# Convolution products added on VectorE before TensorE transposes them; the transposed k in another PSUM bank

## The reference

```python
x = x + tanh(g_xattn) * xattn(ctx, ctx, layernorm(x), ssm_kernel, D)
x = x + tanh(g_ffn) * ffn(layernorm(x), ...)
# xattn, per head h of 8 rows: kv[i,j] = ctx[i] * ctx[j]
#   y[i,j] = causal convolution of kv[i,j] with ssm_kernel[h] (length 512) + D[h] * kv[i,j]
#   out[j] = sum over i of y[i,j] * q[i]
# ffn: y = silu(two-tap convolution); q = silu(y Wq), k = y Wk, v = y Wv, g = y Wg
#   rotary on q and k; a two-way router from v picks the half of q and k that is kept
#   o = (q k^T, masked) v;  out = (silu(g) * normalised o) Wout
```

## Time and profile before

| | |
|---|---|
| median of 3 runs | 1015.58 us (1014.01 to 1015.77) |
| profiled execution, its own time | 1016.0 us |
| its span | 1014.2 us |
| mean granted TensorE clock | 0.981 |
| busy: PE, PEld, DVE, ACT, POOL | 930.4, 790.7, 627.9, 426.9, 672.9 us |

### The profile page before, as it was taken

The page is one execution under the profiler, slowest core; times in us unless marked ns, Lnnn a source line. Parts: engine busy times, 40 slices in busy tenths (PEclk is TensorE's granted clock), DMA queues, the critical chain, the costliest instruction groups (busy, mean ns, idle before and its releaser), DMA issues.

```text
span 1014.2 us, 18862 instructions
## 1 busy us (share of the span) xinstructions
PE 930.4 (92%) x7168; PEld 790.7 (78%) x7168; DVE 627.9 (62%) x1400; ACT 426.9 (42%) x906; POOL 672.9 (66%) x613
## 2 busy tenths in 40 slices
PE   1599999999999999999999999999999999999983
PEld 1488888888888888888888888888888878888862
DVE  4766666657666665666666567666656756656542
ACT  2454444444444444434444443444444444444220
POOL 6677667777666677766667776666777666676321
PEclk9889999999999999999999999999999999999986
DMA  8101222112222210222221022222101222210000
GB/s 275 59 30 44 58 58 58 28 31 58 59 58 58 58 32 28 57 59 58 58 58 32 28 57 59 58 59 58 37 24 56 58 59 58 58 37 9 9 12 21
DMA packets 25992, 52.50 MB, mean 52 GB/s; under 512 B 2544, under 2 KB 3696, under 8 KB 25904
## 3 DMA queue, kind: packets, MB, share of 16 engines
q1 hardware_dynamic: 22304, 46.59, 17.1%
q10 hardware_dynamic: 3600, 4.72, 1.4%
HBM read 42.75 MB, written 8.55 MB: 51 GB/s over the span
## 4 chain that ended last, share of the span: by engine, by line
PE 81%; DMA 5%; issue 4%; POOL 4%; DVE 3%; ACT 2%; SPq 0%; POOLq 0%; ACTq 0%
PE bank L315 34%; PE bank L289 19%; PE bank L276 10%; PE bank L265 8%; DMA x_in<-in_x 4%; PE bank L301 3%; PE bank L347 3%; PE bank L333 3%; ACT gate_sb L583 2%; POOL o_rstd L635 1%; DMA w_all<-in_L_ffn_Wv 1%; POOL rstd L635 1%; POOL rot_b L658 1%; DVE gated L827 0%; POOL kv_low L629 0%
## 5 line engine op out<-in xcount | busy, mean ns | idle before, releaser
L629 POOL TENSOR_TENSOR kv_low<-kv,kv_high 128x576 fp32r<-128x576 f32 x128 | 182.0, 1433 | 162.2 <-ACT kv_high L479 162.2
L289 PE MATMUL bank<-kv_high,toep 128*128 128x512 f32 x640 | 225.2, 409 | 11.0 <-DVE z_terms L732 5.6
L620 POOL TENSOR_TENSOR kv<-kx 128x512 f32<-128x512 f32 x128 | 159.2, 1244 | 6.7 <-DMA const<-shape_consts 6.7
L289 PEld LDWEIGHTS bank<-kv_high,toep 128*128 128x128 f32 x640 | 123.0, 192 | 42.1 <-DVE z_terms L732 12.1
L635 POOL TENSOR_TENSOR o_rstd<-o_ve,minus_half 128x16 f32<-128x16 f32 x32 | 93.1, 2911 | 81.7 <-DVE o_ve L802 81.7
L479 ACT ACTIVATE kv_high<-kv 128x576 fp32r<-128x576 f32 x128 | 87.6, 687 | 101.8 <-POOL kv L623 101.8
L289 PE MATMUL bank<-kv_low,toep 128*128 128x512 f32 x320 | 127.4, 398 | 0.0
L315 PE MATMUL bank<-w_all_high,yT_high 128*128 128x512 f32 (+2 forms) x512 | 120.5, 357 | 1.8 <-DVE gated L827 1.8
L880 DVE TENSOR_TENSOR out_sb<-bank,x 128x512 f32<-128x512 f32 x32 | 22.1, 692 | 159.0 <-PE bank L315 159.0
L276 PEld LDWEIGHTS bank<-const,z_terms 128*128 128x128 f32 x1024 | 113.8, 141 | 5.5 <-ACT qx L468 1.2
L276 PE MATMUL bank<-const,z_terms 128*128 128x128 f32 x1024 | 117.0, 273 | 1.0 <-ACT qx L468 1.0
(11 more groups left out here) (101 smaller groups left out, 1650.5 us busy)
## 6 DMA issues: line engine op xcount, KB each, us to landing
toep<-taps_dram SPq DMA_DIRECT2D x32, 512.0 KB, 7.1
kx<-in_ctx SPq DMA_DIRECT2D x32, 384.0 KB, 7.5
x_in<-in_x SPq DMA_DIRECT2D x32, 256.0 KB
out_x<-out_sb SPq DMA_DIRECT2D x32, 256.0 KB
w_all<-in_L_ffn_Wv ACTq DMA_DIRECT2D x1, 1024.0 KB, 12.6
w_all<-in_L_ffn_Wg ACTq DMA_DIRECT2D x1, 1024.0 KB, 11.3
w_out<-in_L_ffn_Wout ACTq DMA_DIRECT2D x1, 1024.0 KB, 17.1
router<-in_L_ffn_router_w ACTq DMA_DIRECT2D x1, 512.0 KB, 7.3
```

The lines of the kernel that those rows point to most:

```text
L289: ins = nc.tensor.matmul(bank[lc % 2][:, :], toep[:, 1 - p, a, (lc - mc) * P:(lc - mc + 1) * P], kv_p[b][:, 1 - p, mc, 0:FULL], start=(mc ...
L620: eng.tensor_tensor(view(kv[:, c % 2, 0:FULL], [[ROW, NROT], [1, ROW]]), view(kx[:, p, c, 0:ROW], [[0, NROT], [1, ROW]]), view(kx[:, p, c, ...
L629: eng.tensor_tensor(kv_p[1][:, p, c, :], kv[:, c % 2, :], kv_p[0][:, p, c, :].bitcast(F32), ALU.subtract).then_inc(kv_ready[c], 1)
```

## The change

- On DVE, a new function add_halves adds the upper four blocks of z_terms to the lower four, in place: once for chunks 0 and 1 together (right behind u, ahead of line 827), and once each for chunks 2 and 3 (behind multiply of chunk 3, ahead of ratio).
- PE's add_transposed does four transposes a chunk and waits for the sums.
- PE transposes gated ahead of add_transposed, and ACT copies gatedT ahead of the high parts of kv chunks 2 and 3.
- The transposed k goes to bank 7, where gatedT was: PE transposes q first, without waiting for the gate, then waits for gatedT_ready (line 870) and transposes k. The wait for the gate moves to the scores. ACT copies q first, then k. The z transposes wait for the copy of k instead of gatedT_ready.

```diff
@@ tensor: add_transposed
                 for c in range(CH):
-                    if c == 0:
-                        eng.wait_ge(mul_last, h1 + 1)
-                    eng.wait_ge(mul_done[c], h1 + 1)
-                    for i in range(2 * NROT):
+                    eng.wait_ge(sum_done[max(c, 1)], h1 + 1)
+                    for i in range(NROT):
                         ins = nc.tensor.matmul(bank[2][:, c * P:(c + 1) * P], z_terms[:, c, i * ROW:(i + 1) * ROW], ident,
-                                               is_transpose=True, start=(c == 0 and i == 0), stop=(i == 2 * NROT - 1),
+                                               is_transpose=True, start=(c == 0 and i == 0), stop=(i == NROT - 1),
                                                skip_group_check=True)
@@ tensor: scores
+                    eng.wait_ge(qeT_sb, h + 1)
                     eng.wait_ge(keT_sb, h + 1)
-                    eng.wait_ge(qeT_sb, h + 1)
+                    eng.wait_ge(gate_ready, h + 1)
@@ tensor: step
                     eng.wait_ge(z_ready, h + 1)
-                    if can_wait(h - 1):
-                        eng.wait_ge(gatedT_ready, h - 1)
+                    if can_wait(h):
+                        eng.wait_ge(keT_sb, h)
                     transpose4(bank[7], lambda c: z[:, c * P:(c + 1) * P], zT_ps)
...
+                if tail:
+                    eng.wait_ge(gated_ready, h)
+                    if back:
+                        eng.wait_ge(y_conv, h + 1)
+                    else:
+                        eng.wait_ge(keT_sb, h)
+                    transpose4(bank[7], lambda c: gated[:, c * P:(c + 1) * P], gatedT_ps)
                 if front:
                     if pre:
                         eng.wait_ge(qx_ready, h + 3)
                     add_transposed(h + 1)
-                if tail:
-                    eng.wait_ge(gated_ready, h)
-                    if back:
-                        eng.wait_ge(y_conv, h + 1)
-                    transpose4(bank[7], lambda c: gated[:, c * P:(c + 1) * P], gatedT_ps)
...
                     eng.wait_ge(qke_ready, h + 1)
-                    eng.wait_ge(gate_ready, h + 1)
-                    transpose4(bank[5], lambda c: qke[:, RH + 4 * c:RH + 4 * c + 4, :], keT_ps)
                     transpose4(bank[3], lambda c: qke[:, 4 * c:4 * c + 4, :], qeT_ps)
+                    if tail:
+                        eng.wait_ge(gatedT_ready, h)
+                    transpose4(bank[7], lambda c: qke[:, RH + 4 * c:RH + 4 * c + 4, :], keT_ps)
@@ scalar: step (kv_round 2 and 3 now stand behind the copy of gatedT; the copy of qeT ahead of that of keT)
-                if pre:
-                    kv_round(p, 2, h + 2)
-                    kv_round(p, 3, h + 2)
                 if tail:
                     eng.wait_ge(gatedT_ps, h)
...
+                if pre:
+                    kv_round(p, 2, h + 2)
+                    kv_round(p, 3, h + 2)
@@ vector
+            def add_halves(chunks, h1):
+
+                eng.wait_ge(mul_last, h1 + 1)
+                eng.wait_ge(mul_done[chunks.stop - 1], h1 + 1)
+                half = NROT * ROW
+                eng.tensor_tensor(z_terms[:, chunks, 0:half], z_terms[:, chunks, 0:half], z_terms[:, chunks, half:2 * half],
+                                  ALU.add).then_inc(sum_done[chunks.stop - 1], 1)
...
+                if front:
+                    add_halves(slice(0, 2), h + 1)
                 if tail:
                     eng.wait_ge(o_rstd_ready, h)
...
                 if front:
                     multiply(p, 3, h + 1)
+                    add_halves(slice(2, 3), h + 1)
+                    add_halves(slice(3, 4), h + 1)
```

More of the change, by code:

```diff
@@ L194, in flamingo_gated_layer @@
         y_low, gatedT_ready = sem("y_low"), sem("gatedT_ready")
+        sum_done = [sem(f"sum_done{i}") for i in range(CH)]
         (mul_last, y_conv, out_ready, ad_ready, u_ready, th1_ready, rth1_ready, ratio_ready, eps_ready,
@@ L592, in step @@
                 if back:
-                    eng.wait_ge(keT_ps, h + 1)
+                    eng.wait_ge(qeT_ps, h + 1)
                     if can_wait(h):
@@ L596, in step @@
                             eng.wait_ge(attn_ps[r], h)
-                    eng.activation(keT[:, :, :], bank[5][:, :].rearrange("p (c n) -> p c n", c=CH), ACT.Copy
-                                   ).then_inc(keT_sb, 1)
-                    eng.wait_ge(qeT_ps, h + 1)
                     eng.activation(qeT[:, :, :], bank[3][:, :].rearrange("p (c n) -> p c n", c=CH), ACT.Copy
                                    ).then_inc(qeT_sb, 1)
+                    eng.wait_ge(keT_ps, h + 1)
+                    eng.activation(keT[:, :, :], bank[7][:, :].rearrange("p (c n) -> p c n", c=CH), ACT.Copy
+                                   ).then_inc(keT_sb, 1)
             run(eng, step)
```

## The result

The changed kernel takes 1001.27 us (median of 4 runs, 996.31 to 1001.56) against 1015.29 us before: ratio 0.9852, interval [0.9835, 0.9869]. It is 14 us faster, where 27 us slower was forecast.

The account below looks back on a forecast made before the run. PE's program and its waits bound the kernel; after the change POOL's path, 2.2 us longer, decides: 14.33 + 16.1 gives about 30.45 us a step, 0.94 more, +27.3 over 29 steps, -1 at the ends: 1042 us, range 1007 to 1056.

Parts of the forecast that it names:

- the price of the sum of chunks 0 and 1: On DVE behind u: o_rstd on POOL holds the 1024-column sum off until its end, costing 1.1 us a step.
- the forecast step (30.45): One step of the changed kernel: 14.33 us up to T plus 16.1 to the scores, 0.94 over 29.51.
- The small sums: DVE sums of chunks 2 and 3 beside busy POOL: 0.55 us each, 1.1 us on POOL's path, no gain possible.
- part A: Stretch of a step from scores to T (last masks, convolutions, statistics): stays 14.33 us.
- PE alone: PE's own program: 16 fewer transposes save 1.75 us, the dropped gate wait 0.78, together 2.53 us a step.
- v at T + 1.9: PE's start of v, behind the delayed sum and line 827 on DVE: 1.9 us after T instead of 0.78.
- T: The end of POOL's o_rstd, the point where the prediction cuts each step in two.
- the first rival: o_rstd leaves room for the large sum, which costs nothing: step 29.3 us, kernel 1010 us; chance 0.17.
- A wait for line 870: PE, ahead of transposing k, waits 1.55 us for gatedT_ready from DVE, in place of the gate's wait.
- PE waits for the copies ahead of the scores: POOL's rstd ends 2.2 us later, so ACT's copies do too; PE waits 0.9 us a step for them.
- The clock: Rival: PE, idle 3.55 of 30.45 us, loses clock: 1130 us; chance 0.05, shared with another new wait.
- part B: Stretch of a step from T to the scores, 15.10 us before; forecast 16.1, under the first rival 14.95.

Follow-up runs that it names:

- the probe: Changed kernel plus one unused 256-column DVE addition, both inputs in SBUF, asked just after o_rstd starts on POOL: one run, 999.43 us.
- run 6: Changed kernel with the sum of chunks 0 and 1 moved on DVE from behind u to behind the reciprocal, beside POOL's rotation: 1039.17 us, 1.0227 of the kernel before.
- the reordering alone: The change without its sums (32 transposes kept; k in bank 7, new PE and ACT orders): 984.54 us, 0.9702 of the kernel before.
- run 4: Changed kernel with the root of x2 on POOL moved ahead of the low parts of chunks 2 and 3: 962.63 us, 0.9486 of the kernel before.
- Run 7: Kernel of run 4 with the load of x issued ahead of the store of the output: 961.31 us, 0.9466 of the kernel before.

## Why the prediction was wrong

**The step that failed** is the price of the sum of chunks 0 and 1: "I take 1.1 us". It was booked at the upper of its two bounds, 1.1 us; it cost nothing, which was the lower. I chose by the nearest rows, rot_a holding line 832 off to its end and a root waiting for DVE. The second showed that a root that asks while DVE runs waits for it, and I read it the other way round as well, that a running root keeps DVE off. The sum itself denies that, with its 1.21 us inside o_rstd, and so does the probe: 0.17 us into a root, a DVE instruction of two SBUF inputs ran at once.

Of the 1.44 us between the forecast step (30.45) and the measured one (29.01) this is 1.1. The small sums at 0.86 us instead of 1.1 are 0.24, and part A is 0.13 shorter; with roundings that is all of it.

By the Trainium skill (SBUF — State Buffer, "SBUF: two separate sides") the one that starts first has the pair of ports that the two engines share for the whole instruction. Rot_a and the rotation of run 6 agree; the long root does not, with 0.41 us for the probe, and the measurement decides.

**Point by point.**
- PE alone shorter by 2.53 us a step: right. Its busy time fell by 53.4 us, and the reordering alone, for which I had 0.78, made the step 29.51 - 28.52 = 0.99 us shorter.
- v at T + 1.9: wrong, T + 0.86, as the first rival had it.
- The two small sums lengthen POOL's path by 1.1 us, no gain possible: the mechanism right, the size 0.86. The root of x2 ends at 485.21 + 0.54 = 485.75, and T of that step is 502.26 - 28.99 = 473.27: T + 12.48, where before had 518.48 - 506.86 = 11.62.
- A wait for line 870 (now 885) in the gate's place: right, but 0.79 us, not 1.55.
- PE waits for the copies ahead of the scores: right, 1.28 us, forecast 0.9.
- The order on POOL and ACT decides rather than PE's end: right, and proved by run 4.
- The clock did not fall: 0.980 after, 0.981 before, with 2.1 us of PE waiting a step. It did in run 6. The prediction called an idle share of 3.55 in 30.45 us half of 2.96 in 15; it is 0.6 of it.
- The first rival's 29.3 us and 1010 us were 0.3 us a step too long: part B 14.8 us, forecast 14.95, and part A 14.20 for 14.33. Both differences are tenths, and 28 steps of them are 8 us, which carried the result out at the fast end of the range.
- "Part A stays 14.33, as its instructions are the same": wrong by 0.13, most of it the landing of x. In the typical step before, the statistics of x start 500.84 - 500.05 = 0.79 us behind line 780, after the change 496.25 - 495.56 = 0.69 behind line 791, its counterpart. Run 7 against run 4, an edit of the x load alone, takes the same tenth off (median 0.69 for 0.77) and the step 0.11. The few steps of 29.9 us, with x landing later still, went as well: before, the statistics waited for the DMA of x in six places, after in one, at the start.

The chance of 0.17 for this rival was too small for a question of which only one side had been seen in a trace, and the lower end of the range stood on its sum without room for its own rounding.

## What to carry to other kernels

When work goes from a full engine to one with idle time, ask what the third engine beside it is doing in that very stretch: the same addition was free where VectorE was idle beside a GpSimd root, and cost 38 us where VectorE was busy beside a GpSimd rotation. Then follow each engine's path to the next common wait: here a path with 1.27 us to spare became the bound, and moving one small instruction ahead of two long ones on it was worth 39 us, more than the 14 us of the change itself.

## What the runs showed of the hardware

- A GpSimd root (pow, 128 x 16, 2.91 us) does not keep a VectorE instruction with two SBUF inputs off from 0.17 us after its start on (probe 0.41 us, sum 1.21 us, the root still 2.91). Whether it keeps one off in its first 0.17 us was not tried. A root can itself wait for one: 2.01 us for 0.54, at the start of the kernel.
- A GpSimd multiplication or addition of 256 columns and more does: moved beside the rotation, the sum took 1.59 us and the rotation's two halves 1 us more.
- Two SBUF inputs in the same tile, in place, cost VectorE nothing extra: 1024 columns in 1.21 us and 1536 in 1.75, where expand of 1024 took 1.23 with POOL idle.
- TensorE's granted clock fell in ten of the 28 steps of run 6: in one of them to 0.52 over 2 us, behind two waits of 0.77 and 0.96 us. Other steps with the same two waits (0.82 and 0.96 us in the one shown) kept 1.00.
